# POOL normalises the probabilities in front of the rotation's sum, in each step of attention

## The chip, the cores and the metric
The kernel runs on one core of one Trainium2 chip. The metric is the time of one execution on the device, in microseconds (us): 1092.58 in the median of three runs (1091.23 to 1092.96). The core has a matrix engine (TensorE, PE in the profile), VectorE (DVE), ScalarE (ACT), GpSimd (POOL) and SyncE (SP), which issues most of the transfers. Each engine takes its instructions strictly in the order in which they are written, and waits at a semaphore where the code says so.

## The reference
For 16 sequences of 256 tokens with 256 features: x + 0.5 ffn(norm(x)), then x + attention(norm(x)), then x + 0.5 ffn(norm(x)). The feed-forward part has 1024 hidden features and ternary weights. Attention has 16 query heads and 4 key/value heads of 128 features. For each sequence:

```python
q = apply_rotary(x @ Wq, cos, sin)      # t * cos + rotate_half(t) * sin
k = apply_rotary(x @ Wk, cos, sin)
attn = softmax(where(causal, q @ k.T * scale, min))
out = ((attn @ v) * head_scale) @ Wo
```

## The kernel before
The kernel has three stages: the first feed-forward part (to about 190 us), attention (190 to 920 us) and the second feed-forward part. Only attention is touched.

Attention goes through 16 sequences ("batches") of 8 steps. A step `i` handles two query heads, and step number `t` is 8 times the batch plus `i`. A group is four steps (`k` = `i` mod 4 is 0 to 3); in its first step the keys of two key/value heads are projected and rotated as well, in its last step the values are projected. The kernel is software-pipelined by hand: in step `t`, every engine works on the queries of step `t` and on the scores of step `t-2`, later stages lag further. The order on each engine is that in which `batch(b)` writes it; there is no planner.

The rotation of one unit (two heads, 128 partitions by 512 columns, float32) passes three engines. The units are numbered `r`: the keys of a group come first, then the queries of its four steps.

- ACT, `rope_swap` (L587 to L592): waits until the sum of unit `r-2` is done (`wait(act, add, r - 1)`), then copies the projection out of PSUM with its halves swapped, in two copies (L591), to `M2`.
- DVE, `rope_mul` (L1082 to L1090): waits for the same sum and for the swap, then makes two products at L1089, one with the table COS (from PSUM) to `M1`, one with the table SIN, whose two inputs lie in SBUF, in place in `M2`.
- POOL, `rope_add` (L421 to L425): waits for the two products and adds them (two inputs in SBUF) to `QF` or `KF`.

`M1` and `M2` have two buffers, which is why unit `r` waits for the sum of `r-2`: the queries of a first step wait for the sum of the queries of the step before, those of a second step for the sum of the keys, those of a third step for the sum of the first step's queries.

The softmax of step `t-2` runs in step `t`: PE makes the scores (L808, waiting for the sum of that step's queries), DVE adds the mask and takes the maximum (L1108), ACT takes the exponentials with their sums (L619, after its swap of this step), DVE takes the reciprocals (L1124), POOL multiplies the 128x768 exponentials in place by them, in four instructions (`norm`, L434 to L441). ACT casts the result to float16 in the next step, behind that step's exponentials (L626), and DVE takes the rest that the cast left out (L1128, two inputs in SBUF; it waits for the cast). The pair is transposed by DMA and goes to PE.

In a step DVE's order is: the product of the keys' unit if `k` is 0, the maxima (L1108), the product of the queries' unit (L1089), the low part of an output (L1119), the reciprocals of this step's scores (L1124), the rest of the step before (L1128), then the low part of the values if `k` is 3 (L1131). Once per batch it has the residual and the layer norm of an older batch: L1151 at the start of step 0, L1157 and L1160 at the end of step 0, L1166 at the end of step 1, L1171 (two inputs in SBUF) at the end of step 2. POOL has `rows_rstd` (L430, L432) at the end of step 0. ACT's order is: swaps, exponentials, cast, the high part of the values if `k` is 3 (L630), the high part of an output (L635).

Of the kernel before, what the change touches and what calls it, by code (L numbers as in the profile page):

```python
# [52 lines left out]
def program(nc, x, wq, wk, wv, wo, hscale, wu, wg, wd, cos_t, sin_t, out):  # L53
    ctx = ExitStack()
    with ctx:
# [139 lines left out]
        def wait(eng, s, value):  # L195

            if not isinstance(value, int) or value > 0:
                eng.wait_ge(s, value)

        def wait_alone(eng, s, value):  # L200


            if not isinstance(value, int):
                value = eng.to_reg(value)
                eng.wait_ge(consts, 5)
            eng.wait_ge(s, value)
# [37 lines left out]
        def real(b, i, lag):  # L244

            return not isinstance(b, int) or 0 <= PAIRS * b + i - lag < STEPS
# [17 lines left out]
        def norms(work, n, f):  # L264

            return NORMS.get((work, FC * n + f), ())
# [5 lines left out]
        def ends(b):  # L272

            return None if isinstance(b, int) and not 0 <= b - 2 < BATCH else b - 2
# [9 lines left out]
        def batches(eng, body):  # L284
            body(0)
            body(1)
            with eng.Fori(2, BATCH) as b:
                body(b)
            body(BATCH)

        def for_tiles(eng, body):
            body(0)
            with eng.Fori(1, TILES) as n:
                body(n)
# [82 lines left out]
        @block.gpsimd  # L377
        def _(gp):
            gp.memset(NEGHALF[:, :], -0.5).then_inc(neghalf, 1)
            gp.memset(PMAX[:, :], 0.0).then_inc(consts, 1)  # L380
            gp.memset(IDF[:, :], 0.0).then_inc(consts, 1)
            gp.memset(MASK[:, :], 0.0).then_inc(consts, 1)
            gp.wait_ge(consts, 3)
            gp.affine_select(out=IDF[:, :], in_=IDF[:, :], compare_op=ALU.not_equal, fill=1.0, base=0,
                             pattern=[[-1, P]], channel_multiplier=1).then_inc(consts, 1)

            gp.affine_select(out=MASK[:, P:2 * P], in_=MASK[:, P:2 * P], compare_op=ALU.is_ge, fill=MASKED, base=0,
                             pattern=[[-1, P]], channel_multiplier=1).then_inc(consts, 1)

            gp.memset(ONES[:, :], 1.0).then_inc(ones, 1)  # L390
            gp.memset(PM4[:, :], 0.0).then_inc(ones, 1)

            def rstd(q):
                wait(gp, ln_xn, 4 * q)
                wait_alone(gp, ln_mv, 4 * q + 4)
                gp.tensor_scalar(VE[:, :], MV[:, :, 1], 1.0 / LNS ** 2, EPS / LNS ** 2, ALU.mult, ALU.add).then_inc(ln_ve, 1)
                gp.wait_ge(ln_ve, q + 1)
                gp.tensor_tensor(RSTD[:, :], VE[:, :], NEGHALF[:, :], ALU.pow).then_inc(ln_rs, 1)
                if not isinstance(q, int) or q > 0:
                    gp.tensor_scalar(NB0[:, :], MV[:, :, 0], -1.0, None, ALU.mult).then_inc(ln_ve2, 1)  # L400
                    gp.wait_ge(ln_rs, q + 1)
                    gp.wait_ge(ln_ve2, q)
                    gp.tensor_tensor(NB[:, :], NB0[:, :], RSTD[:, :], ALU.mult).then_inc(ln_nb, 1)

            def piece(layer, n, f):

                s = ff[layer]
                gp.wait_ge(s["hh_done"], FC * n + f + 1)
                gp.tensor_tensor(HL[:, f % 4, :], H32[:, f % 2, :], HH[:, f % 4, :], ALU.subtract).then_inc(s["hl_done"], 1)  # L409
                if layer == 0:  # L410
                    for q, _ in norms("stats", n, f):
                        rstd(q)
                if layer == 1 and isinstance(n, int) and (n, f) == (0, EARLY):
                    rows_rstd(BATCH - 1)

            def ffn(layer, n):

                for f in range(EARLY if layer == 1 and isinstance(n, int) and n == 0 else 0, FC):
                    piece(layer, n, f)

            def rope_add(r, m, dst, scored):  # L421

                wait(gp, s_done, scored)
                gp.wait_ge(mul, r + 1)
                gp.tensor_tensor(dst, M1[:, m, :], M2[:, m, :], ALU.add).then_inc(add, 1)  # L425

            def rows_rstd(e):

                wait_alone(gp, a_mv, 2 * e + 2)
                gp.tensor_scalar(VE[:, 0:2], MV[:, 0:2, 1], 1.0 / LNS ** 2, EPS / LNS ** 2, ALU.mult, ALU.add).then_inc(a_ve, 1)  # L430
                gp.wait_ge(a_ve, e + 1)
                gp.tensor_tensor(RSTD[:, 0:2], VE[:, 0:2], NEGHALF[:, 0:2], ALU.pow).then_inc(a_rs, 1)  # L432

            def norm(e, par):  # L434

                wait_alone(gp, rcp, e + 1)
                for hh in range(2):
                    for blk, (lo, hi) in enumerate(BLOCKS):
                        c, lo, hi = 2 * hh + blk, 384 * hh + lo, 384 * hh + hi
                        last = gp.tensor_scalar(EX[:, par, lo:hi], EX[:, par, lo:hi], RI[:, par, c:c + 1], PS, ALU.mult, ALU.mult)  # L440
                last.then_inc(pn, 1)  # L441

            def batch(b):
                for i in range(PAIRS):
                    g, k = divmod(i, 4)
                    u, t = 2 * b + g, PAIRS * b + i
                    r, m = 5 * u + 1 + k, (5 * g + 1 + k) % 2
                    if real(b, i, 0):
                        if k == 0:
                            if isinstance(b, int) and b + i == 0:  # L450
                                gp.wait_ge(ff[0]["down_done"], FC * TILES - 2)
                            rope_add(r - 1, 1 - m, KF[:, g, :], 8 * u - 8)
                        if isinstance(b, int) and b + i == 0:
                            gp.wait_ge(ff[0]["down_done"], FC * TILES)
                        rope_add(r, m, QF[:, i % 2, :], 2 * t - 2)
                    if real(b, i, 2):
                        norm(t - 2, i % 2)
                    if i == 0 and ends(b) is not None:
                        rows_rstd(ends(b))
                    if isinstance(b, int) and b == BATCH and 3 <= i < 3 + EARLY:  # L460
                        piece(1, 0, i - 3)
                    if isinstance(b, int) and (b, i) == (1, 0):
                        rstd(2 * TILES - 1)

            gp.wait_ge(neghalf, 1)
            rstd(0)
            rstd(1)
            for n in range(TILES):
                ffn(0, n)
            batches(gp, batch)  # L470
            for_tiles(gp, lambda n: ffn(1, n))

# [748 lines left out]
```

## Time and profile before

| | us |
|---|---|
| median of three runs | 1092.58 (1091.23 to 1092.96) |
| the profiled execution | 1092.94 |
| its span | 1091.1 |
| PE busy, share of the span | 1070.3 (98%) |
| DVE busy | 925.4 (85%) |
| ACT busy | 815.4 (75%) |
| POOL busy | 713.5 (65%) |

The span is the time from the first to the last instruction in the profile. Busy time is the union of an engine's instructions; matmuls overlap one another and their ends are modelled. A duration of DVE or ACT includes the writing of the results, in which the next instruction may already run: two starts are then closer together than the duration.

### The profile page before, as it was taken

How to read it: one execution, taken by the hardware profiler on the slowest of the kernel's cores; microseconds unless marked ns; L12 is line 12 of the kernel's file. 1: busy time of each engine (PE TensorE's matmuls, PEld its weight loads, DVE VectorE, ACT ScalarE, POOL GpSimd, SP SyncE). 2: the span in 40 equal slices, each digit the busy share in tenths (PEclk: the TensorE clock that was granted, in tenths of full speed). 3: DMA queues.
4: the chain of work that ended last, by engine and by line, in shares of the span. 5: the costliest groups of instructions: out<-in, count | busy, mean ns of one | idle time of the engine just before them, and what ended most of it. 6: DMA issues, size and time to landing. Idle time of an engine off the chain costs nothing.

```text
span 1091.1 us, 26889 instructions
## 1 busy us (share of the span) xinstructions
PE 1070.3 (98%) x8517; PEld 844.1 (77%) x8517; DVE 925.4 (85%) x2313; ACT 815.4 (75%) x2038; POOL 713.5 (65%) x906
## 2 busy tenths in 40 slices
PE   7999999899999999999999999999999999999998
PEld 5556566688888888888888888888888887656565
DVE  6787876899999999999999999999999997433333
ACT  6787887788788787887878878788787785444443
POOL 2566675776777777777777767777677774444443
PEclk9999999999999999999999999999999999999999
DMA  9522332234434344343433434334434343100101
GB/s 347 156 48 40 58 59 37 40 71 89 74 74 76 72 82 82 72 78 65 90 70 72 82 73 81 67 72 82 82 72 76 72 83 73 30 19 19 38 19 38
DMA packets 262166, 79.93 MB, mean 73 GB/s; under 512 B 249328, under 2 KB 260848, under 8 KB 261872
## 3 DMA queue, kind: packets, MB, share of 16 engines
q1 hardware_dynamic: 261696, 79.19, 34.9%
q8 instruction: 20, 0.33, 0.1%
q10 hardware_dynamic: 432, 0.27, 0.1%
q14 instruction: 18, 0.15, 0.0%
HBM read 12.85 MB, written 4.19 MB: 16 GB/s over the span
## 4 chain that ended last, share of the span: by engine, by line
PE 71%; issue 10%; ACT 6%; POOL 6%; DVE 5%; DMA 1%; POOLq 0%; SPq 0%; DVEq 0%; ACTq 0%
PE bank L750 45%; PE bank L808 14%; POOL SCR L409 5%; PE bank L709 4%; PE bank L719 4%; PE bank L739 4%; ACT SCR L619 2%; DVE ARENA L1128 1%; DVE SCR L1089 1%; ACT SCR L492 1%; ACT ARENA L626 1%; DMA X<-in_wg 1%; DVE bank L1108 1%; ACT SCR L507 1%; ACT SCR L517 1%
## 5 line engine op out<-in xcount | busy, mean ns | idle before, releaser
L440 POOL TENSOR_SCALAR SCR<-SCR,RI 128x128 f32<-128x128 f32 (+1 forms) x512 | 309.6, 605 | 44.0 <-DVE RI L1124 3.8
L619 ACT ACTIVATE SCR<-bank,NM 128x128 f32<-128x128 f32 (+1 forms) x512 | 208.2, 419 | 124.3 <-DVE NM L1108 124.3
L425 POOL TENSOR_TENSOR SCR<-SCR 128x512 f32<-128x512 f32 x160 | 203.1, 1269 | 149.4 <-DVE SCR L1089 146.8
L409 POOL TENSOR_TENSOR SCR<-SCR 128x512 f16<-128x512 f32 x128 | 152.7, 1194 | 156.5 <-ACT SCR L507 155.4
L808 PE MATMUL bank<-SCR 128*128 128x128 f32 (+1 forms) x1024 | 193.9, 332 | 4.8 <-ACT SCR L619 4.8
L948 DVE SCALAR_TENSOR_TENSOR SCR<-SCR,CS,bank 128x512 f32<-128x512 f32 x128 | 95.1, 743 | 119.3 <-PE bank L719 98.5
L591 ACT COPY SCR<-bank 64x512 f32<-64x512 f32 x320 | 185.5, 580 | 12.5 <-PE bank L750 6.5
L1128 DVE TENSOR_TENSOR ARENA<-SCR,ARENA 128x768 f16<-128x768 f32 x128 | 187.9, 1468 | 5.5 <-ACT ARENA L626 4.9
L750 PE MATMUL bank<-WOH,ARENA 128*128 128x256 f16 x1024 | 188.3, 273 | 0.8 <-DVE X L1151 0.8
L1108 DVE CUSTOM_DVE_ANT_0 bank<-bank,MASK,SCQ 128x128 f32<-128x128 f32 (+1 forms) x512 | 183.0, 416 | 0.9
L517 ACT ACTIVATE SCR<-bank,SU 128x512 f32<-128x512 f32 x128 | 87.7, 685 | 112.1 <-PE bank L709 110.7
L808 PEld LDWEIGHTS bank<-SCR 128*128 128x128 f32 x1024 | 142.4, 191 | 22.4 <-ACT SCR L619 9.0
L750 PE MATMUL bank<-XX,WQH 128*128 (+1 forms) x1024 | 153.7, 273 | 2.6 <-DVE SCR L1089 2.4
L750 PEld LDWEIGHTS bank<-SCR,ARENA 128*128 128x128 f16 x1536 | 127.3, 98 | 29.9 <-issue 5.3
L750 PE MATMUL bank<-SCR,ARENA 128*128 128x256 f16 (+1 forms) x1536 | 147.6, 246 | 0.9 <-DMA SCR<-ARENA 0.9
L750 PE MATMUL bank<-WOL,ARENA 128*128 128x256 f16 x512 | 139.6, 273 | 0.0
L719 PE MATMUL bank<-XX,TG 128*128 128x512 f16 (+1 forms) x512 | 132.3, 381 | 1.9 <-DVE TG L1018 1.0
L739 PE MATMUL bank<-TD,SCR 128*128 128x256 f16 x1024 | 132.6, 273 | 1.1 <-DVE X L938 0.7
L709 PE MATMUL bank<-XX,TU 128*128 128x512 f16 (+1 forms) x512 | 132.4, 381 | 0.2 <-DVE TU L1018 0.2
L739 PEld LDWEIGHTS bank<-TD,SCR 128*128 128x128 f16 x1024 | 99.5, 98 | 40.0 <-POOL SCR L409 2.6
L1089 DVE TENSOR_TENSOR SCR<-bank,COS 128x512 f32<-128x512 f32 x160 | 109.2, 683 | 5.7 <-ACT SCR L591 4.4
L750 PEld LDWEIGHTS bank<-XX,WQH 128*128 128x128 f16 x1024 | 99.7, 98 | 15.5 <-DVE SCR L1089 4.0
(120 smaller groups left out, 1651.0 us busy)
## 6 DMA issues: line engine op xcount, KB each, us to landing
out<-X SPq DMA_DIRECT2D x7, 512.0 KB, 2.9
X<-in_x SPq DMA_DIRECT2D x1, 2560.0 KB, 11.2
ARENA<-in_wq SPq DMA_DIRECT2D x1, 2048.0 KB, 13.5
ARENA<-in_wo SPq DMA_DIRECT2D x1, 2048.0 KB, 18.6
SCR<-ARENA SPq DMA_TRANSPOSE x128, 3.6
X<-in_x SPq DMA_DIRECT2D x3, 512.0 KB, 9.9
X<-in_wu SPq DMA_DIRECT2D x2, 512.0 KB, 5.8
X<-in_wg SPq DMA_DIRECT2D x2, 512.0 KB, 7.7
```

The costliest lines, as they stand in the source:

```text
L409: gp.tensor_tensor(HL[:, f % 4, :], H32[:, f % 2, :], HH[:, f % 4, :], ALU.subtract).then_inc(s["hl_done"], 1)
L425: gp.tensor_tensor(dst, M1[:, m, :], M2[:, m, :], ALU.add).then_inc(add, 1)
L440: last = gp.tensor_scalar(EX[:, par, lo:hi], EX[:, par, lo:hi], RI[:, par, c:c + 1], PS, ALU.mult, ALU.mult)
L591: last = act.copy(M2[d:d + 64, m, :], PJ[m][s:s + 64, :])
L619: last = act.activation(EX[:, par, 384 * hh + lo:384 * hh + hi], SBK[hh][:, lo:hi], ACT.Exp, bias=NM[:, par, c:c + 1], scale=-1.0, accum_o ...
L709: last = pe.matmul(UB[f % 2][:, :], TU[:, c, f * P:(f + 1) * P], x_tile(n, a, c), start=a + c == 0, stop=a + c == 2)
L719: last = pe.matmul(GB[f % 2][:, :], TG[:, c, f * P:(f + 1) * P], x_tile(n, a, c), start=a + c == 0, stop=a + c == 2)
L739: last = pe.matmul(YB[sub // 2][:, (sub % 2) * D:(sub % 2 + 1) * D], hs[:, f % 4, sub * P:(sub + 1) * P], TD[:, f, :], start=f == 0 and a ...
L750: last = pe.matmul(dst, l(c), r(c), start=start and x == 0, stop=stop and x == len(todo) - 1, skip_group_check=True)
L808: last = pe.matmul(bk[:, lo:hi], QF[:, i % 2, hh * SEQ + blk * P:hh * SEQ + (blk + 1) * P], KF[:, g, kv * SEQ:kv * SEQ + hi - lo], start=b ...
L1108: last = ve.tensor_tensor_reduce(SBK[hh][:, lo:hi], SBK[hh][:, lo:hi], MASK[:, 256 - (hi - lo):256], SCQ[:, 0:1], 3e38, ALU.add, ALU.min, ...
L1128: ve.tensor_tensor(PR[:, par, 768:1536], EX[:, par, :], PR[:, par, 0:768], ALU.subtract).then_inc(p_lo, 1)
```

## The change
On POOL, in each step of attention, the call of `norm` (the four instructions of L440, with the wait for the reciprocals) stands ahead of the calls of `rope_add`. Before it stood behind them. The instructions, their operands and their semaphores are the same, and nothing changes on the other engines.

```diff
                     r, m = 5 * u + 1 + k, (5 * g + 1 + k) % 2
+                    if real(b, i, 2):
+                        norm(t - 2, i % 2)
                     if real(b, i, 0):
                         if k == 0:
                             if isinstance(b, int) and b + i == 0:
...
                         if isinstance(b, int) and b + i == 0:
                             gp.wait_ge(ff[0]["down_done"], FC * TILES)
                         rope_add(r, m, QF[:, i % 2, :], 2 * t - 2)
-                    if real(b, i, 2):
-                        norm(t - 2, i % 2)
                     if i == 0 and ends(b) is not None:
                         rows_rstd(ends(b))
```

## Rows read from the trace of the kernel before

**Rows 1.** Busy time in a stretch: its length, PE, PEld, DVE, ACT, POOL, clock, DMA.
```profile
460.00:860.00 400.00, 400.00 (x3562) 353.39 (x3561) 398.37 (x1060) 325.25 (x916) 293.35 (x394) 1.00 0.40 76
```
**Rows 2.** Timeline of DVE, one L1171 per batch: start, duration, instruction.
```profile
606.35 0.68 DVE L1171 TENSOR_TENSOR NHL<-SCR,NHL 128x512 f16<-128x512 f32 x1
...
651.31 0.68 DVE L1171 TENSOR_TENSOR NHL<-SCR,NHL 128x512 f16<-128x512 f32 x1
```
**Rows 3.** The chain that ended last, two pieces one step apart: start, length, what.
```profile
616.32 1.31 PE bank L808 x8
...
621.24 1.31 PE bank L808 x8
```
**Rows 4.** Timeline of DVE, a second step of a group.
```profile
616.80 0.17 DVE L1124 RECIPROCAL RI<-RS 128x4 f32<-128x4 f32 x1
616.98 1.48 DVE L1128 TENSOR_TENSOR ARENA<-SCR,ARENA 128x768 f16<-128x768 f32 x1
618.38 0.35 DVE L1108 CUSTOM_DVE_ANT_0 bank<-bank,MASK,SCQ 128x128 f32<-128x128 f32 x1
...
619.73 0.68 DVE L1089 TENSOR_TENSOR SCR<-bank,COS 128x512 f32<-128x512 f32 x1
620.33 0.68 DVE L1089 TENSOR_TENSOR SCR<-SCR,SIN 128x512 f32<-128x512 f32 x1
...
621.53 0.16 DVE L1124 RECIPROCAL RI<-RS 128x4 f32<-128x4 f32 x1
```
**Rows 5.** Timeline of POOL, first and second step of the same group.
```profile
611.03 3.05 POOL L440 TENSOR_SCALAR SCR<-SCR,RI 128x128 f32<-128x128 f32 x4
614.16 1.27 POOL L425 TENSOR_TENSOR SCR<-SCR 128x512 f32<-128x512 f32 x1
...
617.73 2.51 POOL L440 TENSOR_SCALAR SCR<-SCR,RI 128x128 f32<-128x128 f32 x4
621.09 1.27 POOL L425 TENSOR_TENSOR SCR<-SCR 128x512 f32<-128x512 f32 x1 [0.85 <-DVE SCR L1089]
```
**Rows 6.** Timeline of ACT, the same stretch.
```profile
611.24 2.37 ACT L591 COPY SCR<-bank 64x512 f32<-64x512 f32 x4
...
617.47 1.17 ACT L591 COPY SCR<-bank 64x512 f32<-64x512 f32 x2
...
620.82 0.84 ACT L626 CAST ARENA<-SCR 128x768 f16<-128x768 f32 x1
```
**Rows 7.** Timeline of DVE, from a fourth step into a first.
```profile
611.67 0.68 DVE L1131 SCALAR_TENSOR_TENSOR ARENA<-bank,ARENA 128x512 f16<-128x512 f32 x1
612.45 0.69 DVE L1089 TENSOR_TENSOR SCR<-bank,COS 128x512 f32<-128x512 f32 x1
```
**Rows 8.** One line each: duration in ns, min/median/max, of its instructions.
```profile
L1128 DVE TENSOR_TENSOR ARENA<-SCR,ARENA x128: 958/1480/1786, 203.2 to 915.3; 128x768 f16<-128x768 f32 x128
...
L1089 DVE TENSOR_TENSOR SCR<-SCR,SIN x160: 670/678/1412, 190.5 to 899.5; 128x512 f32<-128x512 f32 x160
```
**Rows 9.** Timeline at the start of attention, DVE and POOL.
```profile
191.77 1.41 DVE L1089 TENSOR_TENSOR SCR<-SCR,SIN 128x512 f32<-128x512 f32 x1
...
191.37 1.26 POOL L425 TENSOR_TENSOR SCR<-SCR 128x512 f32<-128x512 f32 x1 [1.50 <-DVE SCR L1089]
```
**Rows 10.** Timeline at attention's end, where no rotation is left, DVE and POOL.
```profile
906.28 0.18 DVE L1124 RECIPROCAL RI<-RS 128x4 f32<-128x4 f32 x1 [0.62 <-ACT SCR L619]
906.55 2.69 POOL L440 TENSOR_SCALAR SCR<-SCR,RI 128x128 f32<-128x128 f32 x4 [2.45 <-DVE RI L1124]
907.00 0.99 DVE L1128 TENSOR_TENSOR ARENA<-SCR,ARENA 128x768 f16<-128x768 f32 x1 [0.54 <-ACT ARENA L626]
```
**Rows 11.** Timeline of DVE and POOL, work that comes once per batch.
```profile
633.14 0.86 DVE L1151 SCALAR_TENSOR_TENSOR X<-bank,CW,X 128x256 f32 x2
645.65 1.01 DVE L1166 TENSOR_SCALAR SCR<-X,MV,RSTD 128x256 f32 x2
...
642.07 0.71 POOL L432 TENSOR_TENSOR RSTD<-VE,NEGHALF 128x2 f32<-128x2 f32 x1
```

## Prediction
> **What bounds the kernel now.** I read the table of stretches first, then the engines' timelines over a few groups. In the steady part of attention PE is busy all of 400.00 us, DVE 398.37, ACT 325, POOL 293 [rows 1]. So two engines are full, and POOL is idle a quarter of the time. A batch takes 651.31 - 606.35 = 44.96 us [rows 2]. PE alone would need nearly that: a step with nothing extra takes 621.24 - 616.32 = 4.92 [rows 3], eight make 39.4, and the two projections of keys and two of values per batch add some 1.31 each (twelve matmuls, a third of a step's), 44.6 in all. DVE's step is 621.53 - 616.80 = 4.73 from one reciprocal to the next [rows 4].
>
> POOL has slack in time but not in order. In the trace its sum starts 0.08 us after DVE's sine product ends (620.33 + 0.68, then 621.09), and `norm` comes behind it [rows 4, 5]. The sum's result is waited for by ACT's swap, two units on. Today that wait costs nothing, because the sum is done half a step earlier.
>
> One more thing sets DVE's pace. L1128 takes 1.48 us in most steps, but 0.96 at least [rows 8], and 0.99 where no sum runs beside it [rows 10]. L1089's sine product, also with two inputs in SBUF, took 1.41 instead of 0.68 in the one place where a sum of POOL ran when it started: the sum was over at 192.63, the product at 193.18, 0.55 later [rows 9]. So a DVE instruction with two SBUF inputs is held until POOL's sum is over. It goes the other way too: `norm` takes 2.51 when its start meets L1128, and 3.05 where the keys' sine product meets it as well [rows 5, 7]. Today it is L1128 that is held, by about 0.5 us per step.
>
> **The change, part by part.** Nothing is added or removed. Per step POOL's order becomes: wait for the reciprocals, `norm`, sums. I count from the start of a step's reciprocal on DVE.
>
> 1. *Norm.* Rows 10 show the new order as it stands: reciprocal at 906.28, `norm` from 906.55 to 909.24, with L1128 inside. So `norm` ends at 2.96, where L1128 meets it. In the other case, with L1128 in front of it from 0.17 on, it comes within 0.1 of that.
>
> 2. *Sum.* It can no longer start right after its products, which lie in front of the reciprocal in the same step. It starts at 2.96 + 0.08 (the gap 614.08 to 614.16 [rows 5]) = 3.04 and ends at 4.31. In a first step the keys' sum comes first, the queries' ends at 5.66.
>
> 3. *Who waits.* From the sum's end: 0.08 to the swap (taken as the gap from product to sum), 1.17 for the swap [rows 6], 0.04 to the cosine product (611.24 + 1.17 = 612.41, then 612.45 [rows 6, 7]), then cosine, sine, L1119 until the next reciprocal: 621.53 - 619.73 = 1.80 [rows 4]. The exponentials stand behind the swap on ACT and take about as long (from the swap's end some 1.6, and 0.1 of signals). Together 2.96 + 0.08 + 1.27 + 0.08 + 1.17 + 0.04 + 1.80 = 7.40 from one reciprocal to the next. This loop closes over a single step where the unit two back is the step before: in the first step of a group (its queries wait for the fourth step's sum) and in the second (for the keys' sum). DVE's own path needed 4.73 in a second step. In the third and fourth steps the sum waited for is two steps old and in time.
>
> 4. *First step.* The keys' sine product falls between 2.3 (the keys' swap is ready early) and 3.1 (where the residual's 0.8 [rows 11] comes first); the fourth step's sum wants to start at 3.04. If DVE is first, the sum or `norm` loses about 0.5. If POOL is first, sine ends at 4.31 + 0.55 = 4.86, the next instruction starts at 4.78, the maxima take 1.35 (619.73 - 618.38 [rows 4]) and 1.80 follows: 7.93. Either way the step takes 7.9.
>
> 5. *Second step.* 7.4: its sine product comes at 6.2, when both sums are over.
>
> 6. *Third step.* The exponentials of the second step ended late, and the cast stands behind them, so L1128 starts at 0.72 (906.28 to 907.00 [rows 10]), the next instruction 0.90 later at 1.62, maxima to 2.97, cosine, sine at 3.57: the sum runs from 3.04 to 4.31. Sine ends at 4.86, L1119 starts at 4.78, reciprocal at 5.38. In the first half of a batch L1166 stands before the maxima (0.94 [rows 11]); sine then comes at 4.51, free, and the reciprocal at 5.71.
>
> 7. *Fourth step.* L1128 goes at 0.17, is done with at 1.07, maxima to 2.42, sine at 3.02, and the sum at 3.00 to 3.04: the two start within what I can resolve. Sum first: 5.38. Sine first: 4.22, but then the sum ends late, holds the next L1128, and I put 4.5. I take the mean, 4.9. In the first half L1171 follows L1128 and holds `norm` 0.6 more, which shifts both: 5.9 or 5.1, mean 5.5.
>
> Sum of a batch: 7.9 + 7.4 + 5.7 + 5.5 = 26.5 for the first half and 7.9 + 7.4 + 5.4 + 4.9 = 25.6 for the second, 52.1 against 44.96, so +7.1 us. The rotation and `norm` both stand in 126 of the 128 steps; the first group has only part of the loop, so I count 15.5 batches: +111 us. On the profiled execution's 1092.94 that gives 1204; this execution lies 0.4 us above the median of the runs shown, so it holds for that too. With the sum always first in step 7 a batch is 53.0 and the time 1218, with sine always first 51.3 and 1191.
>
> What hides what: L1128's gain of 0.5 per step is in these sums, and is worth little, as it sits in front of a wait in two of four steps. PE, at 44.6 per batch, is late nowhere; scores are ready when the maxima want them (a sum's end at 4.31 or 5.66, the maxima of that step more than one step later). PT's transposes start earlier or with the same lag. `rows_rstd` comes behind two sums instead of behind `norm`; its reader L1166 stands a step later. At worst its L432 (0.71 [rows 11]) meets the second step's sine product at 6.2 and holds it about 0.45: between 0 and 7 us over 15.5 batches; I take 0, since no row shows a conflict with so small an instruction.
>
> The rule that bears on this is in the Trainium skill, SBUF — State Buffer, "SBUF: two separate sides": DVE and GpSimd share one pair of ports under an exclusive lock, held for a whole instruction by whichever starts first, and a DVE instruction takes part if it runs in a two-port mode or has two SBUF inputs. The trace agrees for L1128, for the sine product and for `norm` [rows 8 to 10]. Taken to the letter it makes L432 hold sine too (the 7 us above), and lets L1166, a tensor-scalar on float32 in SBUF, delay `norm` in a third step, after which sine meets the sum there: some 0.3 us per batch, 5 us. By the rule the sum would be about 1216, by the rows alone 1204.
>
> **Rivals.**
> - *Only the loop costs, the sine products are not held* (the row of 1.41 is a single one, at a start where much is uneven). Third steps are then 2.97 + 1.80 = 4.8 and 5.7, fourth 4.2 and 4.8, first 7.4: a batch of 49.1, +4.1, so 1157. Against it: L1128 is held in nearly all steps by the same sum. 0.10.
> - *`norm` goes first and L1128 behind it.* `norm` is then four instructions in about 1.95, the loop 0.7 shorter in two steps of four; with sine held as before, 52.1 - 2.8 = 49.3, 1160. Rows 10 speak against it: `norm` took 2.69 though it started 0.45 before L1128. 0.06.
> - *Faster.* L1128 is no longer held (0.49 per step), DVE's step falls to about 4.2, and PE alone sets the pace: 44.6 per batch, -0.36, times 15.5: 1087. It decides where a group fits into PE's 22.3 us: with sine not held the third and fourth steps take 4.8 and 4.2, so the two loop steps may take 6.65 each, the sum must be over 3.6 us after the reciprocal and `norm` 2.2 after it. Rows 10 have 2.96, and it needs sine free as well. 0.03.
> - *No difference*: POOL's slack swallows the new order and DVE's hold moves from L1128 to sine, 1093. For it: POOL is idle a quarter of the time. Against it: that slack lies in front of the sums, not behind. 0.03.
> - *More than the sums say*: PE is now idle for some 7 us of 52 in pieces of one to two, and its granted clock, 1.00 here [rows 1], could fall to the lower level. A step of 4.92 would take 9.8 at half the clock; if that hit one step in ten, each 3 us longer, it is +38 on top, 1242. Or L1166, L432 and late exponentials add up to 1 us more per batch, 1220. 0.13 for both.
>
> **How the numbers follow.** My forecast, loop and held sine products, has 0.65: 1204, and 1185 to 1225 on its own. The rest is the rivals' 0.35. The range runs from 1152, which takes in the first two rivals, to 1232. What a measurement can tell from no change is about 0.2%, 2.2 us: faster 0.03, same 0.03, slower 0.94.
>
> **What would show it.** In the changed profile POOL's L425 is no longer released by DVE's L1089, and L440 is by the reciprocals (L1124) in most steps. ACT's L591 is released by POOL's L425 in two steps of four, about 2 and 3 us long, and DVE waits for L591 at L1089. L1128's median falls from 1480 to about 990 ns; L1089's sine product has a second cluster at 1.3 to 1.8 us. PE shows gaps, its busy time stays near 1070 (no less work), its share falls under 92%. In the timeline the four steps of a group last about 7.9, 7.4, 5.5 and 5. The prediction is wrong if L591 waits for PE or for nothing (no loop), if sine stays at 0.68 everywhere (no holding), or if `norm` ends well before 2.9 after the reciprocal.

## The result, and the profile after

The changed kernel takes 1190.03 us in the median of four runs (1188.57 to 1191.12), against 1092.77 for the kernel before on the same chip: a ratio of 1.0893 (95% interval 1.0880 to 1.0906), 97 us slower. Forecast were 1204 us as one number and 1185 to 1225 for the mechanism that was expected; the whole range, with the rivals in it, was 1152 to 1232.

The page of the kernel after: busy time by engine, then three of its groups (line, engine, operation, tiles, count, then busy us, mean ns, idle us before and what ended it).
```profile
PE 1105.4 (93%) x8517; PEld 857.5 (72%) x8517; DVE 912.7 (77%) x2313; ACT 815.4 (69%) x2038; POOL 716.2 (60%) x906
...
L440 POOL TENSOR_SCALAR SCR<-SCR,RI 128x128 f32<-128x128 f32 (+1 forms) x512 | 306.1, 598 | 274.9 <-DVE RI L1124 245.4
L591 ACT COPY SCR<-bank 64x512 f32<-64x512 f32 x320 | 185.5, 580 | 198.4 <-POOL SCR L425 173.8
...
L1089 DVE TENSOR_TENSOR SCR<-bank,COS 128x512 f32<-128x512 f32 x160 | 109.7, 686 | 97.3 <-POOL SCR L425 65.3
```
No engine is full any more. POOL waits for DVE's reciprocals (245.4 us in all) and ACT for POOL's sums (173.8 us), and DVE needs ACT's swapped copy for its products: three engines stand in one ring.

The views of single lines in the kernel after (durations in ns, min/median/max); the last row is from that of L425 and says who waited for it (us, times).
```profile
L1128 DVE TENSOR_TENSOR ARENA<-SCR,ARENA x128: 919/958/1271, 202.4 to 1013.5; 128x768 f16<-128x768 f32 x128
...
L1089 DVE TENSOR_TENSOR SCR<-SCR,SIN x160: 669/681/1711, 190.8 to 997.9; 128x512 f32<-128x512 f32 x160
...
  ACT SCR L591: 173.8, 62
```
These answer to [rows 8]. L1128's median fell from 1480 to 958 ns: in most steps POOL's sum no longer holds it (14 of its 128 instructions take over 1.1 us, 125 did before). The sine product now reaches 1711, and 56 of its 160 instructions take over 0.9 us, against one before. The swap waited 62 times, twice in each of 31 groups.

The timelines of a second step in the kernel after, to be laid beside [rows 4 to 6]; DVE, POOL, ACT.
```profile
623.52 0.15 DVE L1124 RECIPROCAL RI<-RS 128x4 f32<-128x4 f32 x1
...
628.99 0.69 DVE L1089 TENSOR_TENSOR SCR<-bank,COS 128x512 f32<-128x512 f32 x1 [2.95 <-POOL SCR L425]
629.60 0.68 DVE L1089 TENSOR_TENSOR SCR<-SCR,SIN 128x512 f32<-128x512 f32 x1
...
630.80 0.17 DVE L1124 RECIPROCAL RI<-RS 128x4 f32<-128x4 f32 x1
```
```profile
623.84 2.57 POOL L440 TENSOR_SCALAR SCR<-SCR,RI 128x128 f32<-128x128 f32 x4 [3.95 <-DVE RI L1124]
626.50 2.48 POOL L425 TENSOR_TENSOR SCR<-SCR 128x512 f32<-128x512 f32 x2
```
```profile
627.79 1.17 ACT L591 COPY SCR<-bank 64x512 f32<-64x512 f32 x2 [3.65 <-POOL SCR L425]
```
The ring can be read off. From the reciprocal at 623.52 it goes to `norm`, which ends at 626.41 (2.89 later), to the sums from 626.50 (2.98), the swap at 627.79 (4.27), the cosine product at 628.99 (5.47) and the next reciprocal at 630.80 (7.28).

From the starts of DVE's reciprocals I take each step's length, as the median over the batches between 450 and 900 us of the profile; step `i` ends with its own reciprocal (steps 0 and 4 are the first steps of the two groups, 1 and 5 the second ones):

| us | 0 | 1 | 2 | 3 | 4 | 5 | 6 | 7 | batch |
|---|---|---|---|---|---|---|---|---|---|
| before | 7.31 | 5.80 | 5.65 | 5.33 | 6.71 | 4.73 | 4.72 | 4.71 | 44.95 |
| forecast | 7.9 | 7.4 | 5.7 | 5.5 | 7.9 | 7.4 | 5.4 | 4.9 | 52.1 |
| after | 8.19 | 7.29 | 5.61 | 5.66 | 7.76 | 7.29 | 5.38 | 4.08 | 51.26 |

### The profile page after: what moved, and what is told of

The parts are those of the page before. It is cut to its first block, busy times and chain, and to the rows that moved or that the text cites. A ratio compares the mean times of both kernels' runs of the same rounds, so it can differ in the third digit from the quotient of the medians.

```text
span 1189.3 us, 26889 instructions
## 1 busy us (share of the span) xinstructions
PE 1105.4 (93%) x8517; PEld 857.5 (72%) x8517; DVE 912.7 (77%) x2313; ACT 815.4 (69%) x2038; POOL 716.2 (60%) x906
## 3 DMA queue, kind: packets, MB, share of 16 engines
HBM read 12.85 MB, written 4.19 MB: 14 GB/s over the span
## 4 chain that ended last, share of the span: by engine, by line
issue 27%; POOL 24%; PE 19%; DVE 17%; ACT 11%; POOLq 1%; DVEq 0%; ACTq 0%
POOL SCR L440 10%; POOL SCR L425 9%; DVE SCR L1089 7%; POOL SCR L409 5%; DVE bank L1108 5%; ACT SCR L619 4%; PE bank L750 4%; PE bank L709 4%; PE bank L719 4%; PE bank L739 3%; PE bank L808 3%; ACT ARENA L626 2%; DVE NM L1108 2%; DVE ARENA L1119 1%; ACT SCR L591 1%
## 5 line engine op out<-in xcount | busy, mean ns | idle before, releaser
L440 POOL TENSOR_SCALAR SCR<-SCR,RI 128x128 f32<-128x128 f32 (+1 forms) x512 | 306.1, 598 | 274.9 <-DVE RI L1124 245.4
L591 ACT COPY SCR<-bank 64x512 f32<-64x512 f32 x320 | 185.5, 580 | 198.4 <-POOL SCR L425 173.8
L808 PE MATMUL bank<-SCR 128*128 128x128 f32 (+1 forms) x1024 | 207.1, 345 | 70.2 <-ACT SCR L619 68.5
L808 PEld LDWEIGHTS bank<-SCR 128*128 128x128 f32 x1024 | 144.2, 195 | 102.8 <-ACT SCR L619 77.6
L425 POOL TENSOR_TENSOR SCR<-SCR 128x512 f32<-128x512 f32 x160 | 209.7, 1318 | 13.7 <-DVE SCR L1089 3.6
L750 PE MATMUL bank<-WOH,ARENA 128*128 128x256 f16 x1024 | 193.4, 277 | 0.0
L750 PEld LDWEIGHTS bank<-SCR,ARENA 128*128 128x128 f16 x1536 | 135.7, 103 | 33.9 <-issue 3.9
L750 PE MATMUL bank<-SCR,ARENA 128*128 128x256 f16 (+1 forms) x1536 | 159.0, 257 | 0.7 <-DMA SCR<-ARENA 0.7
L1089 DVE TENSOR_TENSOR SCR<-SCR,SIN 128x512 f32<-128x512 f32 x160 | 152.6, 954 | 0.0
L1128 DVE TENSOR_TENSOR ARENA<-SCR,ARENA 128x768 f16<-128x768 f32 x128 | 125.8, 983 | 21.2 <-ACT ARENA L626 21.0
```

The lines of the kernel that those rows point to most:

```text
L591: last = act.copy(M2[d:d + 64, m, :], PJ[m][s:s + 64, :])
L750: last = pe.matmul(dst, l(c), r(c), start=start and x == 0, stop=stop and x == len(todo) - 1, skip_group_check=True)
L808: last = pe.matmul(bk[:, lo:hi], QF[:, i % 2, hh * SEQ + blk * P:hh * SEQ + (blk + 1) * P], KF[:, g, kv * SEQ:kv * SEQ + hi - lo], start=b ...
L1089: last = ve.tensor_tensor(two(dst), two(src), tb[:, :].unsqueeze(1).to_broadcast([P, 2, SEQ]), ALU.mult)
```

## The experiments

Three theories stand against each other. *Loop and holds* is that of the prediction: in a group's first and second steps the swap waits for a sum of the step before, which `norm` and through it the reciprocals hold up; in the others POOL's sum holds DVE's sine product. (A step is "in the ring" where the first of these sets its length, and a product is "held" where it starts beside a sum of POOL and its record is longer for that.) Rival A: the loop alone costs. Rival B: the holds alone cost. The table gives all runs that have a time: the median, the ratio to the kernel before on the same chip with its 95% interval, and the us per batch in the steady part. The diffs are relative to the changed kernel.

| run | us | ratio to before | batch |
|---|---|---|---|
| sine from PSUM | 1171.2 | 1.0712 (1.0694 to 1.0730) | 49.4 or 50.7 |
| third buffer | 1136.1 | 1.0393 (1.0375 to 1.0410) | 48.06 |
| both | 1103.8 | 1.0096 (1.0079 to 1.0113) | 45.84 |
| keys' sum first | 1120.8 | 1.0246 (1.0227 to 1.0265) | 46.83 |
| first step only | 1166.0 | 1.0673 (1.0658 to 1.0688) | 49.0 or 50.3 |
| fourth step only | 1118.5 | 1.0238 (1.0224 to 1.0252) | 46.70 |
| middle steps only | 1093.1 | 0.9999 (0.9990 to 1.0008) | 45.07 |
| second step only | 1092.5 | 0.9998 (0.9989 to 1.0007) | 45.00 |
| half of norm | 1127.9 | 1.0314 (1.0297 to 1.0332) | 47.38 |
| before, half of norm | 1092.1 | 0.9987 (0.9977 to 0.9997) | 44.97 |
| keys' sum first, third buffer | 1103.2 | 1.0087 (1.0071 to 1.0104) | 45.80 |
| the same, sine from PSUM | 1082.6 | 0.9899 (0.9883 to 0.9916) | 44.62 |

**Sine product from PSUM.**
```diff
-((M1[:, m, :], PJ[m][:, :], COS), (M2[:, m, :], M2[:, m, :], SIN))
+((M1[:, m, :], PJ[m][:, :], COS), (M2[:, m, :], PJ[m][:, :], SIN))
```


> The changed kernel, but the sine product reads its first input from PSUM (the projection) instead of the swapped copy in SBUF, so it has one SBUF input. Left out: the rotation's swap of halves no longer enters the result. Same waits. My theory (a loop over one step in a group's first and second steps, and sine products held by POOL's sum in the others): the holds go, the loop stays. A batch then takes 7.4 + 7.3 + 5.6 + 4.9 in its first half and 7.4 + 7.3 + 4.8 + 4.1 in its second, 48.8 us instead of 51.26, so about 1152 us (1140 to 1165). Rival A, the loop alone costs: still 1190. Rival B, the holds alone cost: 1090.

1171 us, 19 less than the changed kernel: neither rival A's 1190 nor rival B's 1090, and 6 us above my range. Its steps are 7.93, 7.32, 5.63, 4.98, 7.37, 7.36, 4.69 and 5.29 (4.20 to 5.44). The second steps and step 4 stay in the ring at 7.3 to 7.4; step 6, held in the changed kernel, falls from 5.38 to 4.69, and step 3 from 5.66 to 4.98. No sine product took over 0.7 us. Of the miss, 0.6 us per batch is there in every batch (49.4 instead of 48.8, most of it in step 0), and a further 1.1 to 1.3 in the longer batches, whose step 7 takes 5.28 to 5.44 instead of 4.20; the last section has more on these.

**Third buffer.** Five units per group, three buffers, dealt so that none waits for the step before.
```diff
+SLOT = (1, 2, 0, 2)   # buffer of the queries of step k; the keys' is 0
+FREE = (4, 2, 2, 1)
-wait(act, add, r - 1)
+wait(act, add, r - free)        # the same in rope_mul
```


> The changed kernel with a third buffer for the two products, dealt out so that no unit waits for a sum of the step before. My theory: the loop over one step goes, ACT's swaps wait for no sum any more, the sine products are still held in about every second step: a batch of 46 to 48 us, 1105 to 1140 us in all, 1120 as one number. Rival A, the loop alone costs: 1087 to 1093, PE sets the pace. Rival B, the holds alone: still about 1190.

1136 us, in my range, 16 over its number, and neither rival A's 1087 to 1093 nor rival B's 1190: 54 of the 97 us come back. No swap waits for a sum any more. A third mechanism shows, which the prediction had called harmless ("PE is late nowhere"). DVE, POOL and PE in step 6 of this kernel:
```profile
642.31 0.68 DVE L1093 TENSOR_TENSOR SCR<-SCR,SIN 128x512 f32<-128x512 f32 x1
...
647.26 0.36 DVE L1112 CUSTOM_DVE_ANT_0 bank<-bank,MASK,SCQ 128x128 f32<-128x128 f32 x1 [2.33 <-PE bank L812]
```
```profile
642.32 3.74 POOL L429 TENSOR_TENSOR SCR<-SCR 128x512 f32<-128x512 f32 x2
```
```profile
646.20 1.57 PE L812 MATMUL bank<-SCR 128*128 128x128 f32 x8 [1.78 <-POOL SCR L429]
```
In a first step, here step 4, two sums stand behind `norm`. They start together with a sine product and end at 646.06. PE's scores (L812 here, L808 before) have waited 1.78 us for the second sum, and DVE's maxima in step 6 2.33 for the scores. Over the whole run the maxima waited 42.1 us for scores, in 31 waits; in the changed kernel 2.4 us, in 3 waits, since the ring is longer and hides it.

**Both.** 

> Third buffer and sine product from PSUM together (the swap of halves does not enter the result). My theory and both rivals: nothing of the loss is left, PE sets the pace at 44.6 to 45.0 us per batch: 1087 to 1093 us. If something else in the new order costs (an idle PE at the lower clock, POOL too late for the scores), it stays above 1100.

1103.8 us, 11 above my range: nearly all is back, but not all, as the last sentence of the expectation has it. 45.84 us per batch are 0.9 above before. Two waits for POOL's sums are left: in the 360 us from 500 on, PE's scores waited 16 times for L429 (2.7 us in all) and ACT's swap 8 times (3.5 us in all). I took the place of the queries' sum, third in POOL's order in a first step, for the cause; the last experiment tests that.

**Keys' sum first.**
```diff
+if k == 0: rope_add(r - 1, 1 - m, KF[:, g, :], 8 * u - 8)
 norm(t - 2, i % 2)
-if k == 0: rope_add(r - 1, 1 - m, KF[:, g, :], 8 * u - 8)
 rope_add(r, m, QF[:, i % 2, :], 2 * t - 2)
```


> The changed kernel, but in a group's first step the keys' sum stands ahead of the normalisation and only the queries' sum behind it. My theory: the second step's swap no longer waits (that sum is done a step's half earlier), the step falls from 7.3 to 5.4 in the second half of a batch and to 5.8 in the first, and the third step's L1128 starts without the wait for the cast: 4 to 5 us less per batch, 1110 to 1140 us, 1122 as one number. The first step's loop stays. Rival A (loop) expects the same or more; rival B, the holds alone: about 1190.

1120.8 us (forecast 1122, rival B 1190). The steps are 7.78, 5.34, 5.29, 5.56, 7.73, 5.39, 4.08, 5.65: the second steps fell from 7.29 to 5.34 and 5.39, the first ones stayed in the ring (7.78 and 7.73). Rival B is out.

**The order changed in a part of the steps.** In each run `norm` stands in front only if `k` is 0; 3; 1 or 2; 1.
```diff
-if real(b, i, 2):
+if real(b, i, 2) and k == 0:        # the other runs: k == 3, k in (1, 2), k == 1
     norm(t - 2, i % 2)
 ...
+if real(b, i, 2) and not (k == 0):
+    norm(t - 2, i % 2)
```


> The changed order in a group's first step alone; the other three have the order of before. My theory: the loop is there only through the keys' sum, so the second steps take 7.3 as in the changed kernel instead of 5.8 and 4.7, the others stay: +1.5 + 2.6 = 4.1 us per batch, 1156 us (1145 to 1165). A theory by which every step pays its share of the loss of 97 us (holds of the sine product, or POOL itself being late) expects a quarter, 1117.

> The changed order in a group's fourth step alone. My theory: the loop is there only through the fourth step's sum, the first steps go from 7.3 and 6.7 to 8.2 and 7.8, the others stay: +1.9 us per batch, 1123 us (1115 to 1130). Every step its share: 1117, so this run tells little by its total, and by its steps: the loss must stand in the first steps.

> The changed order in a group's second and third steps, where no unit of the next step waits for the sum. My theory: no loop, only holds of the sine product against gains of L1128: a step of 4.1 followed by one of 5.6 instead of 4.7 twice, 5.4 and 5.6 instead of 5.6 and 5.3: +0.35 us per batch, 1098 us (1091 to 1104). Every step its share: 1141.

> The changed order in a group's second step alone. My theory: L1128 is free there and the sine product comes just ahead of the sum: a step of 4.1 instead of 4.7 and of 5.4 instead of 5.6, after which PE is the bound at 44.6 per batch: 1089 us (1086 to 1094), the only order so far that could beat the kernel before. Every step its share: 1117.

| us | 0 | 1 | 2 | 3 | 4 | 5 | 6 | 7 |
|---|---|---|---|---|---|---|---|---|
| first step only | 7.94 | 7.30 | 5.65 | 5.32 | 6.70 | 7.30 | 4.72 | 5.29 |
| fourth step only | 7.90 | 5.80 | 5.65 | 5.33 | 7.86 | 4.72 | 4.73 | 4.72 |
| middle steps only | 7.30 | 5.81 | 5.35 | 5.56 | 6.51 | 4.72 | 4.19 | 5.65 |
| second step only | 7.84 | 5.81 | 5.34 | 5.32 | 6.70 | 4.72 | 4.19 | 5.08 |

Against before, the first step's order costs 73 us, the fourth's 26, the middle ones' nothing. The cost stands in the step after: 5.80 and 4.73 became 7.30 where the keys' sum was moved, 7.31 and 6.71 became 7.90 and 7.86 where the fourth step's was. The fourth step's run is in its range (1118.5 for 1123). The first step's is 10 us above its number and 1 above its range: a batch takes 49.0, as expected, or 50.3, and the 1.3 more stand in a step 7 of 5.3 to 5.4 and the step 0 of 7.94 behind it (the medians in the table mix both kinds). That 73 and 26 come to 99, near the change's 97, is therefore in part chance: without these longer batches the two would be some 63 and 26, by my estimate, and the 8 us that are left would be the changed kernel's own holds (51.26 per batch, against 44.95 + 4.05 + 1.75 = 50.75). The middle steps show the trade that was expected, 4.19 then 5.65 for 4.72 twice; it cost 0.1 us per batch instead of 0.35, which this measurement cannot tell from nothing. The second step alone did not gain: 4.19 instead of 4.72 came back as 5.08 and 7.84 later. I had this run at 1089, and 44.6 per batch was not reached. What it lacks I read only from its list of waits, and have not tested: once per batch L1130, which is L1128, waits 0.6 us for the cast, the cast as long for `norm`, and the maxima wait 0.4 us for PE's scores.

**Half of norm.** A dose: the ring must shorten by what is left out.
```diff
 wait_alone(gp, rcp, e + 1)
-for hh in range(2):
+for hh in range(1):
```


> The changed kernel with two of the four instructions of norm (left out: the normalisation of the second head of each pair). My theory: the loop is shorter by what they take, 1.0 us, so the second steps fall from 7.3 to 6.3, the first from 8.2 and 7.8 to 6.9, the third and fourth lose their holds (the sum is over when sine comes): 46.0 us per batch, 1109 us (1100 to 1120). If POOL's place in the order did not set the time, half of its work would still not bring back 80 of the 97 us: a theory by which only the holds count expects 1150 or more.

> The kernel before with the same two instructions left out. My theory: POOL's work is on no path there, no change, 1090 to 1095 us. If POOL's work itself is near the bound, it gets faster by some us.

The second steps fell from 7.29 to 6.30, both, as forecast, and the same work left out of the kernel before moves it by 0.1% (1.2 us, with an interval of 0.3 to 2.5). So it is not POOL's work but its place. In total 1128, 19 over my number and 8 over my range: steps 0 and 2 were 7.38 and 6.53 instead of 6.9 and 5.6. In step 2 there is a hold that I had not counted, in every batch; DVE, then POOL:
```profile
617.54 0.57 DVE L1166 TENSOR_SCALAR SCR<-X,MV,RSTD 128x256 f32 x1
...
618.04 1.43 DVE L1166 TENSOR_SCALAR SCR<-X,MV,RSTD 128x256 f32 x1
```
```profile
618.05 1.27 POOL L425 TENSOR_TENSOR SCR<-SCR 128x512 f32<-128x512 f32 x1
```
L1166 reads one tensor only, and yet its second instruction, 0.5 us long where no sum is near, took 1.43 and ended at 619.47, after the sum's end at 619.32.

**Everything taken away.** Keys' sum first and third buffer, then the sine product from PSUM as well; the edits are those above.

> The changed kernel with the keys' sum ahead of norm and the third buffer. My theory: neither of the two loops over one step is left, nor the wait of the first step's scores for a sum that comes second; only holds of the sine product remain, in steps in which PE has some room: 45.0 to 46.0 us per batch, 1093 to 1109 us, 1098 as one number.

> The same with the sine product's input from PSUM (the swap of halves does not enter the result). My theory: nothing of the change is left on a path, PE sets the pace: 1088 to 1094 us. The 10 us that third buffer and sine from PSUM together still cost were the queries' sum of a first step, third in POOL's order there, for which PE's scores waited; if they stay (1100 or more), that reading is wrong.

1103.2 us, in my range and 5 over its number, and 1082.6 us. The second is below the kernel before, by 1.0%, and below my range (1088 to 1094): I had taken PE's 44.6 per batch for it, which it meets (44.62), but stated the time too near to that of before. By the reciprocals' starts, 14 batches took 5.6 us less in all, the first batch 4.0, and attention began 2.0 us earlier; why the last two are so I have not looked into. Its busy time in a stretch, and a part of its chain that ended last; the last fence is from the chain of the kernel before:
```profile
500.00:860.00 360.00, 360.00 (x3229) 321.84 (x3227) 331.40 (x961) 295.27 (x830) 265.88 (x356) 1.00 0.40 76
```
```profile
607.53 1.31 PE bank L814 x8
608.84 3.61 PE bank L756 x36
612.45 1.31 PE bank L814 x8
```
```profile
603.53 1.64 PE bank L808 x8
```
PE never pauses, and DVE is down to 331 of 360 (92%, against 99.6% in [rows 1]). PE's busy time is full in the kernel before as well [rows 1], but there one of the eight sets of scores in a batch takes 1.64 in the chain, and here none takes more than 1.31: that is the 0.33 between 44.95 and 44.62. The run before this one differs only in where the sine product reads: the holds cost 20.6 us there. *Both* differs from this one only in that the keys' sum stands behind `norm`, which costs some 21 us, twice the 10 that I had named; so it is the order of the sums that *Both* still paid for. No version with the right rotation beat the kernel before; the middle steps' and the second step's order equal it. A version that keeps PE's 44.62 and still feeds the swapped half into the result was not found.

## Why the prediction was right

*The bound before.* DVE was full because L1128 was held, and PE nearly full at 44.6 per batch: the last experiment, without holds, has 44.62.

*Parts 1 to 3 of the prediction, the ring.* 7.40 was worked out, 7.28 measured; 0.07 of the difference is in `norm` (2.89 instead of 2.96 to its end), the rest between the sum's start and the swap. The ring closes where the buffers said it would: third buffer, keys' sum first and the two single-step runs take it away or add it in the steps named, and the swap's waits are 62. In the steady part they were 1.8 and 3.7 us long, the forecast 2 and 3.

*Parts 4, 6 and 7, the holds.* They were predicted from one row (0.55 after the sum's end [rows 9]). In a step 0 of the changed kernel the sum runs from 643.56 to 644.83, and the sine product starts at 643.66 and ends at 645.37, 0.54 after the sum. All 56 sine products of over 0.9 us in that trace end 0.54 to 0.56 after the sum beside them.
```profile
640.42 1.27 DVE L1128 TENSOR_TENSOR ARENA<-SCR,ARENA 128x768 f16<-128x768 f32 x1
...
643.66 1.71 DVE L1089 TENSOR_TENSOR SCR<-SCR,SIN 128x512 f32<-128x512 f32 x1
```
```profile
639.05 1.82 POOL L425 TENSOR_TENSOR SCR<-SCR 128x512 f32<-128x512 f32 x1
640.97 2.51 POOL L440 TENSOR_SCALAR SCR<-SCR,RI 128x128 f32<-128x128 f32 x4
643.56 1.27 POOL L425 TENSOR_TENSOR SCR<-SCR 128x512 f32<-128x512 f32 x1
```
The third step, forecast at 5.71 in the first half of a batch and 5.38 in the second, took 5.61 and 5.38.

*The term that was off* is part 7, the tie in the fourth step. I had taken the mean of both orders, 4.9 us; in the steady part DVE is first in the second half of every batch. Step 7 takes 4.08, the sum is late (1.82 instead of 1.27), holds the next L1128 (1.27), and step 0 pays 0.3: 8.19 for 7.9. In the first half POOL is first: 5.66 for 5.5. All together a batch takes 51.26 instead of 52.1, and 0.84 times 15.5 is 13 of the 14 us between 1204 and 1190. The prediction's own figure for DVE always first, 1191, lies so near by luck, since DVE is first in one half only and step 0 pays for it.

*Two signs that did not come.* PE's busy time was to stay near 1070 us and its share to fall under 92%; they were 1105 and 93%. About a dozen moments at the lower clock, of 3 to 4 us each, would lengthen it by some 20 us (my estimate, half of each); the rest of the 35 I have not looked into.

*What hides what.* "PE is late nowhere" held for the changed kernel, but only because the ring covered it: with the ring gone the scores waited up to 1.78 us in a step. L432 does not hold the sine product: in step 1, L432 runs from 654.28 to 654.99, and the product starts at 654.54 and takes 0.68; the same pair stands in 14 batches, and the product takes 0.68 in each. So the 7 us that the letter of the lock rule gave (the Trainium skill, SBUF — State Buffer, "SBUF: two separate sides") are not there for an instruction of two elements per partition. For L1166, held in the run with half of norm (1.43 instead of 0.5), the rule's word on two-port modes would be a reason; no run shows in which mode it ran. In the changed kernel L1166 met only `norm`, which ended 2.95 after its reciprocal, the sine product missed the sum (0.68), and the step was 5.61: the 5 us are not there either.

*The rivals.* Loop alone (1157), `norm` first with L1128 behind (1160), faster and no difference are all out: each needs the sine product at 0.68, `norm` done by 2.2, or no wait at L591. *More than the sums say* (1242 and 1220) did not come either: the lower clock appeared, but a steady batch was as long without it.

## What to carry to other kernels

An engine that is idle a quarter of the time may still have the one order that works: before moving a wait forward in its queue, follow every instruction now behind it to its readers, and count how many steps of buffering lie between; with one step the wait closes a ring, and its whole length is then the step's length. Where instructions of two engines hold each other up, as here POOL's sum and DVE's instructions with two SBUF inputs, list which pairs overlap before and after: freeing one (L1128, 0.5 us) may put another one (the sine product, up to 1.0 us) in its place. To tell such parts apart, change the order in one step of the pattern at a time and compare the lengths of all steps.

## What the runs showed of the hardware that was not expected

The granted clock of TensorE fell to its lower level for a moment, at most once per batch in the steady part, and in two kernels the batches in which it did were longer. In the run with the first step's order changed, stretches of 3 us (length, then PE's busy time first, granted clock third from the end), and two stretches of a batch's length, the first without such a moment and the second with one:
```profile
512.00:515.00 3.00, 2.12 (x20) 1.66 (x17) 0.22 (x2) 1.01 (x2) 2.85 (x4) 1.00 0.69 131
515.00:518.00 3.00, 1.86 (x10) 1.38 (x11) 2.33 (x5) 2.98 (x11) 1.52 (x3) 0.96 0.00 0
518.00:521.00 3.00, 3.00 (x19) 2.33 (x18) 3.00 (x11) 2.88 (x12) 2.19 (x4) 0.50 0.40 78
...
550.00:599.00 49.00, 45.68 (x403) 39.53 (x401) 43.02 (x120) 36.55 (x104) 32.96 (x45) 1.00 0.37 70
599.00:649.00 50.00, 47.02 (x400) 40.19 (x398) 42.87 (x120) 36.24 (x103) 32.64 (x45) 0.97 0.36 68
```
PE had pauses of about a microsecond in each of two stretches, then 3 us at 0.50 (1.2 GHz instead of 2.4). Behind them DVE's maxima wait for PE's scores, in step 7:
```profile
523.94 0.36 DVE L1110 CUSTOM_DVE_ANT_0 bank<-bank,MASK,SCQ 128x128 f32<-128x128 f32 x1 [0.59 <-PE bank L810]
```
Batches with such a drop took 50.2 to 50.3 us, those without 49.0, in the same run; with sine from PSUM 50.6 to 50.7 against 49.4. In the eleven batches of the first run between 327 and 875 us the drop and the longer step go together each time: the seven with a drop have a step 7 of 5.26 to 5.40, the four without one 4.72. Similar pauses without a drop behind them are there too (PE busy 0.99 of the 3 us from 564 on), and what decides between the two is not shown. In the changed kernel the drop is there as well (its mean clock is 0.978, against 0.998 before), but a batch takes 51.26 with and without it. There a batch is 6.6 us longer than PE's 44.62, and I take this slack for the reason. The prediction had named the clock as what could add 38 us; in the changed kernel it added nothing in the steady part.
